# Moving the router's choice, GpSimd's splits of weights and one transpose at the end of the first attention stage

## The reference

```python
    x = x + jnp.tanh(g_xattn[0]) * _L0_xattn_ref(_layernorm(x, axis=-1), ctx_512, ...)
    x = x + jnp.tanh(g_ffn[0]) * _L0_ffn_ref(_layernorm(x, axis=-1), ...)
# in _L0_ffn_ref:
        probs = jax.nn.softmax(x @ Wr + br, axis=-1)
        w, idx = jax.lax.top_k(probs, K)                  # E = 8 experts, K = 2
        combine = jnp.einsum('tk,tke->te', w, jax.nn.one_hot(idx, E, dtype=x.dtype))
        base_h1 = x @ W1 + b1
        t1 = jnp.einsum('td,erd->ter', x, A1)
        l1 = jnp.einsum('ter,efr->tef', t1, B1) * SCALING
        a = gelu_new(base_h1[:, None, :] + l1)
        ca = a * combine[:, :, None]
        mix = ca.sum(axis=1)
        t2 = jnp.einsum('tef,erf->ter', ca, A2)
        l2 = jnp.einsum('ter,edr->td', t2, B2) * SCALING
        out = mix @ W2 + combine.sum(-1, keepdims=True) * b2 + l2
```

## Time and profile before

| | us |
|---|---|
| median of three runs | 1347.72 |
| lowest and highest of them | 1345.67, 1349.27 |
| the profiled execution | 1349.41 |
| its span in the trace | 1347.6 |

### The profile page before, as it was taken

How to read it: one execution, slowest core, us unless ns; L and a number is a source line. 1 busy time by engine, 2 the same in 40 slices (tenths; PEclk the granted TensorE clock), 3 DMA queues, 4 the chain that set the end, 5 groups by cost and what they waited for, 6 DMA issues and landing times.

```text
span 1347.6 us, 20320 instructions
## 1 busy us (share of the span) xinstructions
PE 1322.7 (98%) x7404; PEld 1070.1 (79%) x7404; DVE 933.3 (69%) x1805; ACT 517.2 (38%) x1569; POOL 403.3 (30%) x461
## 2 busy tenths in 40 slices
PE   7999999999999999999999999999999999999999
PEld 6888888888887788778887888788876677788877
DVE  5766676675775868775778667866888887746533
ACT  3544455454464321231123111311127777822220
POOL 4212322231356252201111111114416865630000
PEclk9999999999999999999999999999999999999999
DMA  8755454443672232210221012112334655555431
GB/s 298 236 164 157 148 165 141 165 146 128 197 218 75 75 87 72 81 39 17 70 83 47 18 45 91 32 50 72 104 102 126 197 180 194 168 192 160 144 114 55
DMA packets 131655, 163.51 MB, mean 121 GB/s; under 512 B 15436, under 2 KB 85196, under 8 KB 131556
## 3 DMA queue, kind: packets, MB, share of 16 engines
q1 hardware_dynamic: 131556, 162.22, 38.1%
HBM read 109.74 MB, written 52.43 MB: 120 GB/s over the span
## 4 chain that ended last, share of the span: by engine, by line
PE 85%; DVE 6%; ACT 4%; DMA 3%; issue 1%; SPq 1%; POOL 0%; DVEq 0%; ACTq 0%; POOLq 0%
PE bank L118 84%; ACT P L124 2%; PE bank L121 2%; DVE AH L130 1%; DVE STG L130 1%; DMA pscr<-STG 1%; SPq L170 1%; ACT PTV L124 1%; DVE XR L140 1%; DMA PTV<-pscr 1%; DVE AH L127 1%; ACT STG L124 1%; DVE sm L146 1%; DMA STG<-in_Wqr_dram 0%; DVE XT L130 0%
## 5 line engine op out<-in xcount | busy, mean ns | idle before, releaser
L118 PE MATMUL bank<-XT,AR 128*128 128x512 f32 x1152 | 280.1, 393 | 0.8 <-DVE XT L130 0.7
L118 PE MATMUL bank<-AR 128*128 128x512 f32 x1056 | 259.1, 396 | 0.7 <-DVE AR L130 0.7
L118 PEld LDWEIGHTS bank<-XT,AR 128*128 128x128 f32 x1152 | 214.0, 188 | 49.1 <-issue 1.7
L124 ACT ACTIVATE STG<-bank,b1c 128x512 f32<-128x512 f32 x128 | 88.3, 690 | 387.5 <-PE bank L118 320.3
L118 PEld LDWEIGHTS bank<-AR 128*128 128x128 f32 x1056 | 194.0, 188 | 47.2 <-issue 3.2
L118 PE MATMUL bank<-AR,CT 128*128 128x512 f32 x768 | 191.2, 392 | 0.0
L118 PE MATMUL bank<-AR,AH 128*128 128x512 f32 x768 | 185.8, 390 | 0.0
L127 DVE CAST AH<-STG 128x512 fp32r<-128x512 f32 x192 | 91.9, 479 | 112.8 <-PE bank L118 98.9
L118 PEld LDWEIGHTS bank<-AR,AH 128*128 128x128 f32 x768 | 143.6, 188 | 30.7 <-issue 1.1
L118 PEld LDWEIGHTS bank<-AR,CT 128*128 128x128 f32 x768 | 140.2, 188 | 27.0 <-issue 0.4
L127 POOL CAST BA<-STG 128x256 fp32r<-128x256 f32 x64 | 30.7, 479 | 397.7 <-PE bank L118 242.8
(11 more groups left out here) (143 smaller groups left out, 1820.4 us busy)
## 6 DMA issues: line engine op xcount, KB each, us to landing
XR<-scr SPq DMA_DIRECT2D x64, 256.0 KB, 3.0
pscr<-PYZ SPq DMA_DIRECT2D x30, 512.0 KB, 2.9
PYZ<-pscr SPq DMA_DIRECT2D x120, 128.0 KB, 2.9
XR<-in_x_dram SPq DMA_DIRECT2D x32, 256.0 KB, 3.6
XR<-lscr SPq DMA_DIRECT2D x128, 64.0 KB, 2.0
scr<-XR SPq DMA_DIRECT2D x32, 256.0 KB, 2.1
pscr<-STG SPq DMA_DIRECT2D x16, 512.0 KB, 2.6
PTV<-pscr SPq DMA_DIRECT2D x64, 128.0 KB, 2.8
```

Source lines behind the costliest of these rows:

```text
L118: return self.e.matmul(o, w, x, start=start, stop=stop, skip_group_check=True) if self.e else Nothing()
L124: return self.e.activation(o, x, func, **kw) if self.e else Nothing()
```

## The change

Three orders are changed; no instruction is added or removed. In `vector`, at u = 32, `router_b(0)` comes ahead of `pv1(31)`. In `tensor`, at u = 33, the masks' transpose comes ahead of `wo1(31, (0,))`. In `gpsimd`, from u = 32 on, `ba_split` comes ahead of `w_split`, and GpSimd waits for `ms_ok[0]` before the first of them.

```diff
@@ tensor
                     stA0(0)
-                    wo1(31, (0,))
                     mask_turn(0, 7)
-                    wo1(31, (1,))
+                    wo1(31, (0, 1))
@@ vector
                 if u == 32:
                     router_turn(0)
                     router_a(0)
+                    router_b(0)
                     pv1(NU - 1)
-                    router_b(0)
@@ gpsimd
+                if u == 32:
+                    e.wait_ge(*ms_ok[0])
+                if u >= 32:
+                    ba_split(u - 32)
                 if u >= 28:
                     for f in fl_step[u - 1]:
                         w_split(f, u < 32)
-                if u >= 32:
-                    ba_split(u - 32)
```

## The result

| | before | changed |
|---|---|---|
| median of 22 runs, us | 1347.75 | 1351.07 |
| lowest and highest | 1345.66, 1349.78 | 1347.77, 1354.58 |
| the profiled execution | 1349.41 | 1351.15 |
| its span | 1347.6 | 1349.4 |

The changed kernel takes 1.0027 of the time of before (95% interval 1.002 to 1.0035): 3.3 us slower. The forecast was 1347.4, no change, and 1351.07 lies just outside the range's upper end of 1351.0. One later run of before, timed beside e5 to e8, took 2205.55 us at a granted clock of 0.557 and is in no comparison.

The account below looks back on a forecast made before the run. PE bounds the kernel, with 85% of the chain that ended last. A 2.1 us gain at the masks less 2.0 lost at the ports gave -0.1, leaned to -0.3: 1347.4 from a median of 1347.72, range 1344.0 to 1351.0.

Parts of the forecast that it names:

- the shorter choice and the earlier transpose: Choice on DVE takes 4.36 us, so PE's masks' transpose needn't wait; last twelve `wo1` matmuls start 2.1 us sooner.
- the 1.84: PE's gap before the masks' transpose, put down to DVE's late MM; 1.84 us, expected to close.
- the ports: DVE's steps F = 0 and 1 meet GpSimd's late splits; PE loses 2.0 us at `stB(1)` and `stB(2)`.
- The forecast of 2.4: DVE time lost beside 3.31 us of GpSimd's TENSOR_TENSOR on BA(2) and f = 8, at a factor of 0.73.
- Its full price, 4.5 us: By the skill's lock rule GpSimd's casts block DVE too: all 4.92 us count, PE loses 4.5, 2.4 net.
- that BA(3) costs nothing and that nothing follows: Step F = 2: BA(3) landed at 457.2, split 458.4 to 459.0, before `stA1(3)` at 459.85; no later cost named.
- With a net of nothing it waits for nothing: `stA1(3)`: with gain and loss cancelling, PE doesn't wait for BA(3); 2.1 us earlier it would wait 0.6 to 1.2.
- Rival 3: Slower, 25%: GpSimd's casts block DVE too, net +1.1 us, 1348.8; marked by over 2.5 us of DVE time lost.
- signs of being right: Transpose gap gone, 2.1 us gained, GpSimd idle about 3 us before BA(1) and BA(2), long DVE operations, PE idle +2.
- the 0.40: PE's gap before the six matmuls at 450.86 (`stB(1)` and `stA1(2)`), put down to ACT; 0.40 us.
- those of being wrong: Matmuls at `stB(2)` still 2 us earlier, PE waiting over 1 us for BA in F = 1 to 4, or MM late.
- -2.1 to +2.0: Outer net effects of the four rivals on the whole time, widened by about 1.6 us of run spread each side.

Follow-up runs that it names:

- e5: Changed kernel, with each low-rank load up to F = 3 issued on SP ahead of the large weights it had stood behind; 1346.65 us, 0.9996 of before.
- e8: The changed kernel timed again, nothing altered; 1350.70 us, 1.0024 of before.
- e6: Changed kernel without GpSimd's wait for the masks, `ba_split` still first; 1346.25 us, 0.9990 of before, and timed again 1346.15, 1.0001.
- e7: Changed kernel with GpSimd's old order and its wait for the masks placed between the splits of f = 6 and `ba_split(0)`; 1347.25 us, 0.9995 of before.
- e2: Kernel before with GpSimd's part alone (the wait, and `ba_split` ahead of `w_split`); 1356.53 us, 1.0068 of before.
- e4: Changed kernel with `ba_load(3)` issued on SP ahead of the four stores; 1349.79 us, 1.0021 of before.
- e13: The kernel before, unaltered, in a second single profiled execution; its stretch from block 0's router turn to block 1's took 145.5 us.
- e1: Kernel before with PE's and DVE's parts alone, GpSimd in its old order without the wait; 1353.08 us, 1.0041 of before.
- e11: Kernel before with only PE's and DVE's parts, again, in a single profiled execution; stretch from block 0's router turn to block 1's 148.24 us.
- e9: The changed kernel, unaltered, in one more single profiled execution; 1353.52 us.

## Why the prediction was wrong

**Right: the shorter choice and the earlier transpose.** Forecast 2.1 us by the last twelve matmuls of `wo1`, measured 2.07. DVE's timeline of the changed kernel has the choice from its first operation to its last on MM as

```profile
424.27 0.19 DVE L130 TENSOR_TENSOR rt<-bank,brb 128x32 f32<-128x32 f32 x1 [1.52 <-PE bank L121]
...
428.05 0.19 DVE L130 TENSOR_TENSOR MM<-MM 128x32 f32<-128x32 f32 x1
```

3.97 us, where I had said 4.36; CT is split before `wo1` wants it. Its worth against the typical execution of before is smaller, though: the 1.84 was one execution's alignment. Two others had 0.50 + 0.22 and 0.43 + 0.23 to win; from the start of `stA0(0)` to the last twelve matmuls of `wo1` they took 8.12 and 8.04 us against 7.15 in the changed kernel, so 0.9 in all. I read one trace of before and took its gap for the kernel's.

**Right in mechanism, a little small: the ports** (those that VectorE and GpSimd share, by the prediction's reading). Forecast 2.0 of PE's time at `stB(1)` and `stB(2)`; measured 2.45 (from 2.07 ahead to 0.38 behind). DVE's timeline of the changed kernel, then GpSimd's:

```profile
448.82 1.52 DVE L127 CAST AH<-STG 128x512 fp32r<-128x512 f32 x1
450.38 0.98 DVE L130 TENSOR_TENSOR AH<-STG,AH 128x512 fp32r<-128x512 f32 x1
451.28 1.51 DVE L127 CAST AH<-STG 128x512 fp32r<-128x512 f32 x1
452.82 0.69 DVE L130 TENSOR_TENSOR AH<-STG,AH 128x512 fp32r<-128x512 f32 x1
```

```profile
448.43 1.62 POOL L130 TENSOR_TENSOR AR<-STG,AR 128x512 fp32r<-128x512 f32 x1
450.00 0.81 POOL L127 CAST AR<-STG 128x512 fp32r<-128x512 f32 x1
450.89 1.62 POOL L130 TENSOR_TENSOR AR<-STG,AR 128x512 fp32r<-128x512 f32 x1
```

DVE's four operations take 4.70 where 2.24 would do with GpSimd idle, so 2.46 is lost. The forecast of 2.4 was for all that meets BA(2) and f = 8, though, and two operations ahead of these grew too (447.04, a cast of 0.84, and 447.92, a subtraction of 0.98): with them DVE lost 3.2. Each of the two long casts ends 0.3 us behind the subtraction that it met (450.34 after 450.05, 452.79 after 452.51). The two subtractions beside GpSimd's casts grew by 0.29 each. GpSimd's own operations grew too, 1.29 to 1.62 and 0.61 to 0.81. The Trainium skill, "SBUF — State Buffer", "Who interferes with whom", has the later engine blocked until the first has ended, casts included. By these ends the trace agrees, the cast as well. Its full price, 4.5 us, did not come.

**Wrong: that BA(3) costs nothing and that nothing follows.** The step that failed is "With a net of nothing it waits for nothing", and there was no term at all behind F = 2. I reckoned BA(3) landed at 457.2 and PE wanting it at 459.85. SP's queue and GpSimd's timeline show what came:

```profile
455.50 0.77 SPq L170 DMA_DIRECT2D STG<-in_A2T_dram  x1
```

```profile
458.61 0.40 POOL L127 CAST BA<-STG 128x256 fp32r<-128x256 f32 x1 [6.10 <-DMA STG<-in_A2T_dram]
```

My times are on the clock of the trace of before, whose `stA0(0)` starts 1.03 later. On it the load was issued at 456.5 behind the four stores, 1.8 later than my 454.7, since the splits of f = 8 ended at 453.5 and not at 451.6. Some 1.6 of these 1.9 is the other half of the meeting with DVE, which I had priced on DVE's side alone: the pair on BA(2) took 1.8 us in place of 1.2, and f = 8 took 5.0 in place of 3.9. And the load released GpSimd 3.11 after its issue, in place of 2.47. PE waited 0.67, and from 0.38 behind it came to 1.5 behind in the steps that follow (473.24, before 472.77): 1.1 lost. The larger omission is what a late start does there: I took the wait at F = 2 for a single event, while split, `w_load`, `ba_load` and trip feed each other in rounds of 8.25 us on average against PE's 8.16 to 8.19. The slack that had hidden long trips was gone up to step F = 8. One long trip in it, at F = 7, cost waits of 1.83 and 0.54, and 3.0 in position (1.5 to 4.49); the split behind it met DVE's mix as well (a cast of 0.83 and a subtraction of 1.05 from 501.14 on, in place of 0.39 and 0.73).

**The ledger.** Against the trace of before that I had read: -2.07 + 2.45 + 1.1 + 3.0 = +4.5, the 4.49 of the stretch. Against a typical execution: -0.9 + 2.45 + 1.1 and 0 to 3.0 for F = 7 and 8, so +2.6 to +5.6. The mean of four stretches of the changed kernel, 150.08, less that of three of before, 145.89, is 4.2. The medians say 3.3. Rival 3 had the sign, and its mark was passed: more than 2.5 us of DVE's time was lost. But by `stB(2)` the net was +0.38 and not its +1.1, the operations beside GpSimd's casts account for 0.6 of the 3.2 that DVE lost, and most of the slowdown came behind, where it had no term.

**The signs.** All that I had named as signs of being right came (the gap closed, the gain of 2.1, the two idle times of GpSimd of 3.35 and 3.27, the long DVE operations, 2.3 more of PE's idle time than the 0.40), and of those of being wrong none: the wait for BA at F = 2 was 0.67, under my 1 us. They ended at F = 4, and the wait of 1.83 is at F = 7.

**The range.** It was made of the terms that I had, -2.1 to +2.0, with 1.6 for the spread. From the median of 1347.72 these give 1344.0 to 1351.3; the upper end of 1351.0 that I wrote is 0.3 too low. A range that held 1351.07 by that would have held it by luck, since +2.0 stood for another mechanism. A ring that can turn a trip's scatter into PE's time was not among them. The ratio of 1.0027 is still within the 0.3% to which I gave 92%, but by other terms than mine. Before such a chance I should have asked of every new exposed wait whether its lateness is worked off or carried.

**What the parts would give.** The best stretch is that of e6 (144.61 twice) and e7 (144.60), 0.9 us below the 145.5 of before. Its total time, 0.9990 and 1.0001 of before, does not resolve so little: that these orders are faster than before is not shown.

**Open.** Why the A2T trip at F = 7 takes 4.2 to 4.3 us in some executions: transfers of instruction code lie in that time, which shows nothing of a cause. That trip was long in e2 as well (4.3), and 2.8 in before, where it had slack.

## What to carry to other kernels

Ahead of moving work on an engine that is mostly idle, find what its end releases: here a later split on GpSimd delayed the load behind it in SP's stream, and so its own next input. Where the rounds of such a loop are as long as the step of its consumer (8.25 against 8.16), a start that is late by a microsecond stays late, and a long transfer in it is paid; where they are shorter (7.78 in e4), it is worked off. Compare the two periods, and leave the loads of small, early wanted data ahead of those that wait. A gap read in one execution may be that execution's alignment of two engines, so read two or three before it is counted as a gain.

## What the runs showed of the hardware

Single small operations of DVE (128x4 to 128x32 elements, 0.15 to 0.2 us) get 1.2 to 1.3 us long beside a GpSimd subtraction, and which of them is hit changes from one execution of the same code to the next (on MM a pair of 1.83 and one of 1.25 in before; a pair of 1.36, 0.41, and 1.24 on w12c in e13).

A stop of PE of about 2 us is sometimes followed by its lower clock level. In e1 the twelve matmuls behind a stop of 1.82 us took 4.62, with a granted clock of 0.75 in the window, between the levels of 1.2 and 2.4 GHz. In e11, the same kernel, PE's timeline has two stops and no fall (the stretches of 148.29 and 148.24 are equal by chance: e1 lost some 1.6 to the clock, e11 1.57 at the transpose, where e1 had no wait):

```profile
433.00 0.61 PE L121 MATMUL bank<-ident,MM 128*24 128x128 f32 x4 [1.57 <-DVE MM L130]
435.25 3.02 PE L118 MATMUL bank<-AR,CT 128*128 128x512 f32 x12 [1.65 <-DVE CT L130]
```

In e2 it fell after stops of 2.42 and 1.82:

```profile
451.00:461.00 10.00, 8.06 (x22) 6.13 (x23) 8.02 (x9) 2.08 (x4) 6.90 (x6) 0.66 0.18 50
```

The four profiled executions of the changed kernel keep 1.00 there. Over its 34 runs, the 20 with a mean clock of 1.000 have a median of 1349.6, and the 14 below it have medians of 1351.6 to 1354.6 by level; before, runs at 1.000 have 1346.0 and those at 0.998 have 1347.9. So falls of the clock belong to the spread of both kernels, and between runs at 1.000 alone the medians still differ by 3.6 us. Where those of the changed kernel can lie, e9 shows (1353.52 us, mean clock 0.997): in windows of 5 us the granted clock is 0.90 and 0.76 from 1025 to 1035 and 0.66 from 1175 to 1180. These are places far from the change, where the kernel before falls too (0.66 at 1025 to 1030 in its first trace, at 1170 to 1175 in e13). What follows the last of the stretches took 491.6 us in e9, and 488.7 to 488.9 in the three executions without a fall.
